# Last expert's first half of tokens by seven block products, with the two layers after it packed into fewer steps

## The reference, cut to what matters

```python
x = x + L0(x)   # two experts of four by sample type, three shared MLPs (relu), gated by the first token
x = x + L1(x)   # 8 experts + 1 shared:  (silu(x @ Wg) * (x @ Wu)) @ Wd, width 1024, weighted per sample
x = x + L2(x)   # per sample: relu(x @ w1 + b1) @ w2 + b2, added to x, layer norm, gamma, beta
x = x + L3(x)   # per sample: x @ W.T + bias, 256 -> 256
```

## Time and profile before

| | us |
|---|---|
| median of 3 runs | 1580.34 (1580.19 to 1582.08) |
| profiled execution, its own time | 1579.02 |
| its span, first to last instruction | 1576.9 |
| TensorE busy | 1569.8 |
| VectorE busy | 1132.5 |
| ScalarE busy | 931.6 |
| GpSimd busy | 674.2 |

### The profile page before, as it was taken

The page is one execution under the profiler, slowest core; times in us unless marked ns, Lnnn a source line. Parts: engine busy times, 40 slices in busy tenths (PEclk is TensorE's granted clock), DMA queues, the critical chain, the costliest instruction groups (busy, mean ns, idle before and its releaser), DMA issues.

```text
span 1576.9 us, 22436 instructions
## 1 busy us (share of the span) xinstructions
PE 1569.8 (100%) x7916; PEld 1339.6 (85%) x7916; DVE 1132.5 (72%) x1685; ACT 931.6 (59%) x1683; POOL 674.2 (43%) x631
## 2 busy tenths in 40 slices
PE   9999999999999999999999999999999999999999
PEld 7888888999988888888888888888888888888898
DVE  6855557788889876776777776776776776657567
ACT  5655555666666666565565666666656666555444
POOL 7865544766786441431432432342342352038000
PEclk9999999999999999999999999999999999999999
DMA  4111105455520000000010010010010010022000
GB/s 161 55 54 54 54 27 184 165 181 180 175 82 27 27 28 27 24 31 27 15 41 28 14 41 27 14 40 28 14 41 27 14 41 27 15 60 77 14 14 28
DMA packets 31012, 85.98 MB, mean 55 GB/s; under 512 B 5030, under 2 KB 10534, under 8 KB 30774
## 3 DMA queue, kind: packets, MB, share of 16 engines
q1 hardware_dynamic: 30310, 83.21, 15.3%
q0 software_dynamic: 304, 1.10, 0.2%
q10 hardware_dynamic: 288, 0.26, 0.1%
HBM read 82.46 MB, written 2.10 MB: 54 GB/s over the span
## 4 chain that ended last, share of the span: by engine, by line
PE 96%; POOL 1%; DVE 1%; DMA 0%; issue 0%; SPq 0%; ACT 0%; ACTq 0%; POOLq 0%; DVEq 0%
PE up L684 13%; PE up L683 13%; PE up L682 13%; PE sum L441 13%; PE sum L443 13%; PE sum L442 13%; PE up L441 4%; PE up L442 4%; PE up L443 4%; PE up L449 2%; PE up L451 2%; PE up L450 2%; DMA raw<-in_shared 0%; DVE gate_inputs L2029 0%; POOL shared_up L1496 0%
## 5 line engine op out<-in xcount | busy, mean ns | idle before, releaser
L1305 ACT ACTIVATE hidden_hi<-up_tile 128x512 fp32r<-128x512 f32 x256 | 161.2, 630 | 189.4 <-DVE up_tile L2147 166.8
L2152 DVE TENSOR_TENSOR hidden_lo<-up_tile,hidden_hi 128x512 fp32r<-128x512 f32 x256 | 197.8, 792 | 44.7 <-ACT hidden_hi L1305 44.7
L2142 DVE TENSOR_TENSOR gate_tile<-up,gate_tile 128x512 f32<-128x512 f32 x192 | 130.0, 687 | 138.9 <-PE up L684 138.4
L682 PE MATMUL up<-x_sums,gate_up 128*128 128x512 f32 x512 | 199.2, 389 | 0.0
L443 PE MATMUL sum<-hidden_hi,down 128*128 128x512 f32 x512 | 199.2, 389 | 0.0
L442 PE MATMUL sum<-hidden_lo,down 128*128 128x512 f32 x512 | 199.2, 389 | 0.0
L684 PE MATMUL up<-x_sums,gate_up 128*128 128x512 f32 x512 | 199.2, 389 | 0.0
L441 PE MATMUL sum<-hidden_hi,down 128*128 128x512 f32 x512 | 199.2, 389 | 0.0
L683 PE MATMUL up<-x_sums,gate_up 128*128 128x512 f32 x512 | 199.2, 389 | 0.0
L2147 DVE TENSOR_TENSOR up_tile<-up_tile,gate_tile 128x512 f32<-128x512 f32 x192 | 184.0, 985 | 2.2
L1298 ACT ACTIVATE gate_tile<-gate_tile 128x512 f32<-128x512 f32 x192 | 119.8, 632 | 90.5 <-DVE gate_tile L2142 88.2
(11 more groups left out here) (332 smaller groups left out, 4007.1 us busy)
## 6 DMA issues: line engine op xcount, KB each, us to landing
raw<-in_experts SPq DMA_DIRECT2D x64, 512.0 KB, 3.3
raw<-in_l SPq DMA_DIRECT2D x51, 512.0 KB, 3.2
raw<-in_shared SPq DMA_DIRECT2D x23, 512.0 KB, 3.3
raw<-in_w SPq DMA_DIRECT2D x8, 256.0 KB, 2.7
x<-in_xT SPq DMA_DIRECT2D x3, 512.0 KB, 9.1
l_stage<-in_l SPq DMA_DIRECT2D x3, 512.0 KB, 4.2
out<-out_stage SPq DMA_DIRECT2D x6, 256.0 KB, 2.2
gate_w<-in_gw POOLq DMA_DIRECT2D x1, 1024.0 KB, 5.1
```

The source lines that it names most:

```text
L682: pe.matmul(out, wh, vh, start=first, stop=False, skip_group_check=True)
L1305: A(hi[:, i], cu[:, i], ACT.Copy).then_inc(hi_done, 1)
L2142: V.tensor_tensor(t, ps, t, ALU.add).then_inc(c_done[m], 1)
L2152: V.tensor_tensor(lo[:, i], cu[:, i], hi[:, i].bitcast(f32), ALU.subtract).then_inc(lo_done, 1)
```

## The change

**Ninth expert.** Its first block of 1024 tokens now goes through `pair_up` and `pair_down` as the other experts do; `PAIR_BLOCKS` has one entry more. Only tokens 1024 to 2047 are left to the plain steps: three jobs in place of five, 24 steps in place of 40. The plain steps read the same weight tiles as the pairs; for the one block (`l21`) which the seven products use only in sums, a tile of its own is filled.

**Units.** There are still five. Units 0 and 1 have their x complete when the last pair is done, units 2 to 4 follow their jobs. `WHEN` is new for all: unit 0 in steps 2 to 13, unit 1 in 3 to 19, unit 2 in 10 to 27, unit 3 in 18 to 34 and unit 4 as before, 16 steps earlier. Unit 1 uses the other pair of PSUM banks. There are three y tiles and two for the squares in place of one each.

**Row sums.** Only unit 2 still has its mean from the row sum; unit 1 takes four matmuls.

**Squares.** For units 0 to 2 ScalarE makes both squares, VectorE only adds them.

**Late weights.** ScalarE has them at steps 1, 1, 3, 3, 4, 5, 6, 7, VectorE's `center_w2` one step ahead of each. GpSimd adds the unit matrix up to three samples ahead of the low parts, and unit 0's power stands between the low parts of the sixth and the seventh sample. `center_b2` is at step 2. Half of the bias rows of L3 are loaded only after unit 1's down product.

```diff
-LAST_JOBS = [(0, BLK), (BLK, BLK), (2 * BLK, BLK), (3 * BLK, S), (3 * BLK + S, S)]
+LAST_JOBS = [(2 * BLK, BLK), (3 * BLK, S), (3 * BLK + S, S)]
+UNITS = [(0, BLK), (BLK, BLK)] + LAST_JOBS
+LAST_STEPS = 8 * len(LAST_JOBS)
+PAIR_BLOCKS = [(e, j) for e in range(NS) for j in range(2)] + [(NS, 0)]
+LATE_AT = [1, 1, 3, 3, 4, 5, 6, 7]
 WHEN = [dict(zip(STAGES, at)) for at in (
-    (9, 10, 11, 11, 11, 11, 12, 12, 12, 13, 13, 13, 13, 14, 14, 14, 15, 15, 16, 16, 17, 18),
-    (17, 18, 19, 19, 19, 19, 20, 20, 20, 21, 21, 21, 21, 22, 22, 22, 23, 23, 24, 25, 25, 26),
-    (25, 26, 27, 28, 28, 28, 30, 30, 30, 31, 32, 31, 32, 34, 34, 35, 35, 36, 38, 38, 39, 39),
-    (34, 34, 35, 35, 35, 35, 37, 37, 37, 38, 39, 39, 40, 41, 43, 43, 45, 45, 46, 48, 46, 50))]
-for u in (0, 3):
+    (2, 2, 4, 4, 4, 4, 6, 6, 6, 7, 7, 7, 7, 8, 8, 9, 9, 10, 12, 12, 12, 13),
+    (3, 6, 8, 9, 9, 9, 11, 11, 11, 12, 13, 12, 13, 15, 15, 15, 16, 16, 18, 18, 19, 19),
+    (10, 11, 14, 15, 15, 15, 17, 17, 17, 18, 19, 18, 19, 21, 21, 21, 22, 22, 24, 24, 26, 27),
+    (18, 18, 20, 21, 21, 21, 23, 23, 23, 24, 25, 25, 25, 26, 27, 27, 29, 29, 30, 32, 30, 34))]
+for u in (0, 1, 3):
     del WHEN[u]["xs"]
...
-        unit_ps = [sums[0], sums[0], sums[0], up_ps[:, 2:4], sums[0]]
+        unit_ps = [sums[0], up_ps[:, 2:4], sums[0], up_ps[:, 2:4], sums[0]]
...
             def gate_up_hi(e, s):
...
                 A(gu[s][:, 0, :, 0:3 * P], raw_pairs(o, 0, 3), ACT.Copy)
+                if e == NS:
+                    A(l21[s][:, 0], raw_pairs(o, 3, 4), ACT.Copy)
                 A(gu[s][:, 0, :, 3 * P:7 * P], ws[s][:, :, 3 * P:7 * P], ACT.Copy).then_inc(w_hi, 1)
...
             def first_square(i):
...
-                A(sq[:, 0, c], y[:, 0, c], ACT.Square).then_inc(sq_first, 1)
+                if i:
+                    act.wait_ge(var_done, i)
+                A(sq_of[i][:, 0, c], y_of[i][:, 0, c], ACT.Square)
+                act.wait_ge(centered, DT * (i + 1))
+                A(sq_of[i][:, 1, c], y_of[i][:, 1, c], ACT.Square).then_inc(sq_first, 1)
...
             for b in reversed(range(B)):
-                hooks.setdefault(late_step(b), []).insert(0, lambda b=b: late_hi(b))
+                hooks.setdefault(LATE_AT[b], []).insert(0, lambda b=b: late_hi(b))
...
-            for b in range(B):
+            pool.wait_ge(consts, 1)
+            for b in range(4):
                 w3_plus_one(b)
-                if b:
-                    late_lo(b - 1)
-            late_lo(B - 1)
-            pool.wait_ge(consts, 1)
+            late_lo(0)
+            for b in range(1, B):
+                late_lo(b)
+                if b + 3 < B:
+                    w3_plus_one(b + 3)
+                if b == 5:
+                    rstd_stage(0)
...
             for b in range(B):
-                hooks.setdefault(late_step(b) - 1, []).append(lambda b=b: center_w2(b))
-            hooks.setdefault(24, []).append(beta_lo_part)
-            hooks.setdefault(9, []).append(center_b2)
+                hooks.setdefault(LATE_AT[b] - 1, []).append(lambda b=b: center_w2(b))
+            hooks.setdefault(16, []).append(beta_lo_part)
+            hooks.setdefault(2, []).insert(0, center_b2)
+            hooks.setdefault(0, []).append(mean_matrix)
```

More of the change, by code:

```diff
@@ L155, in build @@
     ws = [place(f"weight_sums{s}", [P, 2, 7 * P], f32, over=f"gate_up{s}", skip=7 * K1) for s in range(PAIRS)]
-    xst = place("x_row_sum", [P, BLK], f32, over="raw", skip=14336)
-    xsr = [place(f"x_row_sum_parts{r}", [P, 2, BLK], f32r, over="weights", skip=(12 - 4 * r) * K1) for r in range(2)]
+    xst = place("x_row_sum", [P, BLK], f32, over="weights", skip=14 * K1)
+    xsr = place("x_row_sum_parts", [P, 2, BLK], f32r, over="weights", skip=12 * K1)
     cg = place("gate_tile", [P, 3, BLK], f32, over="weights", skip=88 * K1)
@@ L193, in build, with w1_part @@
     w2s = place("w2_sum", [2 * A2, 1], f32, over="shared_sums", skip=small + 896)
[L194 to L198, removed]
+    late_slot = [raw_slot_of(b) for b in range(B)]
+    y0 = place("y0", [P, DT, BLK], f32, over="weights", skip=8 * K1)
+    y1 = place("y1", [P, DT, BLK], f32, over="raw", skip=4 * K1 * late_slot[4])
+    y2 = place("y2", [P, DT, BLK], f32, over="raw", skip=4 * K1 * late_slot[7])
+    y_of = [y0, y1, y2, y1, y2]
+    sq0 = place("squares0", [P, DT, BLK], f32, over="weights", skip=12 * K1)
+    sq1 = place("squares1", [P, DT, BLK], f32, over="raw", skip=4 * K1 * late_slot[5])
+    sq_of = [sq0, sq1, sq1, sq1, sq1]
+    ru0 = place("l2_hidden0", [A2, BLK], f32, over="shared_sums", skip=4 * K1)
+    u0 = place("l2_hidden_r0", [2 * A2, BLK], f32r, over="shared_sums", skip=6 * K1)
+    ru1 = place("l2_hidden1", [A2, BLK], f32, over="raw", skip=4 * K1 * late_slot[6])
+    u1 = place("l2_hidden_r1", [2 * A2, BLK], f32r, over="raw", skip=4 * K1 * late_slot[6] + 2 * K1)
+    ru_of, u_of = [ru0, ru0, ru1, ru1, ru1], [u0, u0, u1, u1, u1]
+    def w1_part(b, h, m):
+        return gu[3][:, h, b // 4, 3 * P + b % 4 * P + m * A2:3 * P + b % 4 * P + (m + 1) * A2]
     ctx = ExitStack()
@@ L282, in last_steps @@
         def last_steps(step, hooks):
-            for T in range(40):
+            for T in range(LAST_STEPS):
                 job = T // FT
@@ L774, in last_up @@
                         b = (0, 1, 3, 2)[f % 2 * 2 + dt]
-                        c = slice(b * P, (b + 1) * P)
-                        last = product(ps, gul[f // 2][:, 0, m, c], gul[f // 2][:, 1, m, c],
+                        wt = [l21[f // 2][:, h, m] if b == 3 else gu[f // 2][:, h, m, b * P:(b + 1) * P] for h in range(2)]
+                        last = product(ps, wt[0], wt[1],
                                        xh[:, dt, tok:tok + N], xl[:, dt, tok:tok + N], dt == 0, dt == DT - 1)
@@ L995, in _ @@
             last_steps(last_step, hooks)
-            for T in range(40, 60):
-                if T < 42:
+            for T in range(LAST_STEPS, ALL_STEPS):
+                if T < LAST_STEPS + 2:
                     last_down(T - 2, S)
@@ L1772, in _ @@
                 mixed_lo_part(NB - 2, dt)
-            for e in range(NS):
+            for e in range(NE1):
                 weight_sums(e, 2)
@@ L2384, in out_stage @@
                 dve.wait_ge(l3_done, 2 * i + part + 1)
+                if i == 1 and not part:
+                    dve.wait_ge(mean_done, 3)
                 if i >= 2 and not part:
                     dve.wait_ge(stored[i % 2], 32 * (i // 2))
+                    dve.wait_ge(small_full, 16 * late_small)
                 V.tensor_tensor(ostage[:, i % 2, q:q + half],
```

265 lines of the change are left out of this document (132 added, 133 removed).

## The result

The changed kernel takes 1591.99 us (median of 4 runs, 1587.88 to 1592.62) against 1580.77 us for the kernel before on the same chip: a ratio of 1.0059, 95% interval 1.0047 to 1.0072. It is slower by 0.59%, some 9 us; the two medians lie 11.2 us apart (0.71%), which is inside the interval. That is above the range of the forecast (1586.0) and far from its 1582.3 us.

The account below looks back on a forecast made before the run. The prediction took TensorE as the bound: -4.99 us of matmuls plus stalls of 2.0, 3.5 and 1.5 us gave +2.0 us, so a median of 1582.3 us against 1580.34 before, range 1576.8 to 1586 us.

Parts of the forecast that it names:

- What bounds the kernel: TensorE, busy 1569.8 of 1576.9 us: each matmul removed is worth its full time, each new wait costs its full time.
- A: Step 8, broadcast of unit 0's scale: TensorE has 7.7 us of work, the chain takes 9.7; stall 2.0 us.
- -4.99 us: Matmul saving: 24 fewer of 512 columns in the ninth expert, 2 more for unit 1's row mean.
- Ninth expert's weights at 0: Extra weight sums, splits and copies for the ninth expert's pairs cost 0 us, bounds 0 to 0.5.
- GpSimd stretches VectorE: Rival: GpSimd's late weights and row sum slow VectorE at A and B; stalls 9.7, 1585 us; chance 0.22.
- B: Steps 9 to 11, unit 1's way down to its hidden layer: stall 3.5 us, 2.5 to 4.5.
- C: The rest, such as waits in steps 17 and 24 and the tail: 1.5 us, bounds 0 and 3.
- The clock falls: Rival: clock drops to 1.2 GHz behind B's wait until step 13, about 5 us more, 1587 us; chance 0.05.
- The sum: -4.99 + 2.0 + 3.5 + 1.5 = +2.0 us: 1581.0 us as the profiled execution, 1582.3 as a median.
- VectorE near 85%: Sign the forecast is right: VectorE near 85% busy in the last 100 us, from 84 of 98 us.

Follow-up runs that it names:

- e_a: Changed kernel with unit 0's variance moved to step 8, its factor to step 9, the seventh and eighth late weights to step 8: 1585.23 us, ratio 1.0022.
- e_wait2: Kernel before, TensorE made to wait in plain step 13 for two small DMAs, one after the other: 1587.23 us, ratio 1.0037.
- e_ab: Changed kernel with both the edits of e_a and those of e_b: 1582.63 us, ratio 1.0006.
- e_ab2: e_ab with ScalarE's copies of the seventh and eighth samples' late weights at step 9, behind unit 0's diagonals: 1584.67 us, ratio 1.0013.
- e_wait1: Kernel before, TensorE made to wait in plain step 13 for one small DMA: 1583.80 us, ratio 1.0011.
- e_nolow: Changed kernel with GpSimd writing zeros in place of the late weights' low parts, the matmuls kept: 1585.77 us, ratio 1.0025.
- e_fill: Changed kernel with twelve unused 256-column matmuls ahead of unit 1's down product in step 11: 1587.75 us, ratio 1.0040.
- e_b: Changed kernel with unit 1's mean and hidden layer made in step 8 in place of 9: 1587.04 us, ratio 1.0031.
- e_ab3: e_ab with the seventh sample's late weights split behind step 8's diagonals and the eighth's at the head of step 9: 1585.38 us, ratio 1.0025.
- e_ab4: e_ab with the seventh sample centred at step 5 and split at step 7, the eighth split at step 11: 1585.63 us, ratio 1.0024.

## Why the prediction was wrong, point by point

**What bounds the kernel** held: in the last part the profiled executions differ by TensorE's matmuls, waits, restarts and clock, but for the 0.7 us behind the last matmul. That a new wait costs its full time was too little: each costs some 0.15 us more at the restart, and several came with a stretch at 1.2 GHz (A in after, e_a, e_wait2).

**-4.99 us** held: 22 matmuls fewer on the page, and the four pairs take 59.84 us without a gap. **Ninth expert's weights at 0** held, with GpSimd at 24.36 us in that window in place of 7.64.

**A** ("VectorE in the same time finishes a tile (0.5), does the residual (1.6) ... Stall 2.0 us") failed in its start, not in its list. It counted VectorE's work from unit 0's l2_down as if VectorE came to it on time and with the durations of a VectorE alone. In the trace it is 3.1 us late, because GpSimd's low parts stretched its operations in steps 1 to 6 (39.51 against 36.45 us without them). The wait is 2.54 us at the squares plus 0.32 at rstd_diag, 2.9 in place of 2.0. Without them it is 1.6 at rstd_diag, as the list says. The rival "GpSimd stretches VectorE" named this mechanism with the right row (1.49 against 0.43 us). It had 0.22, priced as 1 to 1.5 us at A (it came to 1.3), and took the centring as what is stretched. That was (1.05 us in the row shown), and hidden_lo (1.13) and x_lo (0.6) with it. Its total is too small by its own terms: with the 1 us at B and C at its bound the stalls are 10.5 to 11 us, 9.7 was written.

**B** ("Stall 3.5 us, 2.5 to 4.5") held: 3.0 at the down product and 0.2 at the up products of step 11. In this the rival was wrong: unit 2's row sum did fall into B, at 1517.31, but beside an operation with an input in PSUM, and stretched nothing.

**C** (1.5 us) was within its bounds: four waits of 0.28, 0.34, 0.57 and 0.48 us behind 1540, less the 0.2 of before, and 0.7 behind the last matmul, 2.2 us in all.

**"The clock falls. Chance 0.05"** is the step that failed most: the sum has the clock at 1.00 behind its waits, a term put at nothing. The forecast thought of a fall behind B alone, and took the 1.3 us wait of the earlier trace rows, with its clock of 1.00, as evidence for gaps twice as long. The profiled execution has it behind A, 2.5 us, with 1.6 us of loss; e_wait2 makes it in the kernel before with a wait of 2.3 us; and the executions of after with a mean clock of 0.994 or 0.995 take 4 us more than the profiled one. The 5 us given to one fall are three times what one costs in the trace; that they are near the 1.6 and 4 us together is luck. The Trainium skill's rule (TensorE: Matmul & The Clock Gate, the table "Why this matters for your kernels"), that long idle gaps between bursts of matmuls bring the lower clock, is borne out by these rows in its direction; the gap that the page warns of is longer than the 2.3 to 2.5 us that were enough here, and the measurement decides.

**The sum.** The waits that the change adds to the profiled execution, its tail included, are 8.2 us where 7.0 was forecast, and TensorE idle is 14.7 us in all where about 14 was forecast. The waits alone would have given 1583.5 us as a median, well inside the range; as a profiled execution it would have been 1582.2 (the forecast put 1.3 us between the two). The profiled one took 1587.9. Of the 5.7 us between, 1.6 are the low clock behind A, 1.9 the restarts and what was not followed, and 2.4 lie ahead of the last part, 1.5 of them the clock in L0, which has nothing to do with the change (the span's margin gives 0.2 back). The median lies another 4.1 us higher, most likely by more time at 1.2 GHz, of which the place is not shown.

**VectorE near 85%** did not show: from the first plain step to the last down product it is busy for 76.0 of 106.0 us, 72%, where 84 of 98 were forecast. The stretch itself has grown by the waits and the low clock, and VectorE's work was counted 8 us too high, though GpSimd stretched it. The share says little in any case: the waits come from order, not from the load of the whole stretch.

**Left open.** Which executions show a fall behind a given wait, and why the clock stays at 1.00 behind the 3.0 us wait of the profiled one. No execution with a mean clock of 0.994 was profiled, so where its further time at 1.2 GHz lies is not known. The 0.9 us ahead of the first plain step beside the clock in L0 weren't followed. Whether a version beats before is open too: e_ab's 4.4 us of waits are what would have to go, and a schedule in which the late low parts are done ahead of the last expert was not tried.

## What to carry to other kernels

A wait that you put into a TensorE that had been kept busy has a price beyond its length: the restart costs some 0.15 us each time, and the matmuls around its end may run at half speed for 3.4 us or more, so a saving of 5 us should not be bought with two waits of 2.5 to 3. When work on VectorE is packed beside work on GpSimd, lay out the time of both, and count each VectorE operation with two inputs in SBUF as waiting for the GpSimd instruction beside it; those with an input in PSUM, or with only one, keep their times. A stage moved off a busy place must be followed with all that it issues on the other engines: e_ab2 moved ScalarE's copies by one step, ended a wait of 1.8 us, and got one of 3.4 us from the GpSimd work that came with them.

## What the runs showed of the hardware that was not expected

- Behind waits of TensorE of 1.2 us (e_wait1), 1.6 (e_nolow, e_fill) and 1.8 us (e_ab) the granted clock was 1.00. It was at 1.2 GHz for a stretch with waits of 2.3 (e_wait2, e_fill), 2.4 (e_a), 2.5 (after), 2.9 (e_b) and 3.4 us (e_ab2, e_ab3), and also 1.1 us behind one of 1.5 us in e_ab4, which had one of 0.7 us 2.5 us ahead of it. It stayed at 1.00 behind the 3.0 us wait for unit 1's hidden layer in after and in e_nolow. So the length of a single wait does not decide it.
- The low stretch does not begin at a fixed distance from the wait: 1.4 us before the wait's end in e_ab3, 0.1 before it in e_wait2, 1.3 behind it in after, 1.6 behind it in e_b. It lasted 3.4 us in all these profiles but e_ab2 and e_ab3, where it lasted 6.8.
- The clock fell without a wait in L0, behind 24 fp32 matmuls of 8 columns and 8 of 2 columns (3.5 us), in all profiled executions but those of before and e_wait2, whose code there is that of e_wait1. It costs 1.5 us where it lasts 3.4, and in e_nolow and e_ab2 it lasts 6.8. It can be part of why executions of one kernel differ by 2 to 4 us.
- The port conflict shows in single rows: 0.69 to 1.82 us for a subtraction of 512 columns, 0.43 to 1.48 for a centring, 1.65 to 3.98 for four products, and no change for the operations with an input in PSUM and for the one-input reduction (0.41 us throughout).
